# A macaron block with FP4 weights: the decoding of the packed words on 32-bit words instead of 16-bit ones

## The reference, cut to what matters

```python
def dequant_fp4(packed_i32, scales_f16, group_size):   # packed: [out, in/8]
    w = packed_i32.astype(uint32)
    nib = w[:, :, None] >> (arange(8) * 4) & 15        # eight 4-bit codes in a word
    vals = FP4_LUT[nib].reshape(out_f, in_p * 8)       # 0 .5 1 1.5 2 3 4 6, and their negatives
    return vals * repeat(scales_f16.T, group_size, axis=1)

def ffn(x, gate_up_packed, gate_up_scales, down_packed, down_scales):   # inner size 1408
    w_gu, w_down = dequant_fp4(gate_up ...), dequant_fp4(down ...)
    gate, up = split(x @ w_gu.T)
    y = (silu(gate) * up) @ w_down.T
    return y / sqrt(mean(y * y) + 1e-6)

x = X + 0.5 * ffn(layernorm(X), ...)
x = x + attention(layernorm(x), ...)
x = x + 0.5 * ffn(layernorm(x), ...)
```

## Time and profile before

| | |
|---|---|
| median of 3 runs | 2764.01 us (2751.09 to 2766.40) |
| profiled execution | 2762.66 us, its span 2760.8 us |
| mean granted TensorE clock | 0.983 |
| PE busy | 2596.6 us (94%) |
| DVE busy | 1894.5 us (69%) |
| POOL busy | 1574.8 us (57%) |
| ACT busy | 1476.6 us (53%) |

### The profile page before, as it was taken

The page is one execution under the profiler, slowest core; times in us unless marked ns, Lnnn a source line. Parts: engine busy times, 40 slices in busy tenths (PEclk is TensorE's granted clock), DMA queues, the critical chain, the costliest instruction groups (busy, mean ns, idle before and its releaser), DMA issues.

```text
span 2760.8 us, 39357 instructions
## 1 busy us (share of the span) xinstructions
PE 2596.6 (94%) x14559; PEld 1365.0 (49%) x14559; DVE 1894.5 (69%) x3325; ACT 1476.6 (53%) x2823; POOL 1574.8 (57%) x1095
## 2 busy tenths in 40 slices
PE   5799999997998999999999999999999999999997
PEld 3455555554873333333378633333334555555554
DVE  7877777766648777777175487777662777777764
ACT  4366666665222656656622146666665456666664
POOL 4556666665221666666742136666677456666665
PEclk8899999998999999999999999999999999999999
DMA  2002311121122020200050310202003401111101
GB/s 62 1 31 92 126 47 46 46 77 56 36 69 58 4 50 5 63 5 3 15 186 31 79 33 5 48 5 63 5 4 119 175 16 46 47 46 47 46 31 46
DMA packets 75710, 136.32 MB, mean 49 GB/s; under 512 B 18783, under 2 KB 22394, under 8 KB 75390
## 3 DMA queue, kind: packets, MB, share of 16 engines
q1 hardware_dynamic: 75518, 133.81, 15.7%
HBM read 71.12 MB, written 34.34 MB: 38 GB/s over the span
## 4 chain that ended last, share of the span: by engine, by line
PE 69%; DVE 11%; POOL 6%; ACT 4%; issue 4%; SPq 1%; DMA 0%; POOLq 0%; ACTq 0%; DVEq 0%
PE pp L95 54%; PE ps L95 14%; DVE sb L116 6%; POOL sb L104 6%; ACT sb L101 4%; DVE sb L110 3%; SPq L137 1%; DVE sb L104 1%; PE ps L98 1%; DVE sb L107 0%; DMA sb<-sb 0%; PE pp L98 0%; DVE sb L113 0%; DVE sb L122 0%; ACT L101 0%
## 5 line engine op out<-in xcount | busy, mean ns | idle before, releaser
L95 PE MATMUL pp<-sb,sb 128*128 128x512 f32 (+9 forms) x11082 | 2198.1, 440 | 65.7 <-DVE sb L110 17.1
L104 POOL TENSOR_TENSOR sb<-sb,sb 128x512 f32<-128x512 f32 (+6 forms) x1078 | 1567.2, 1475 | 1182.8 <-PE pp L95 442.5
L95 PEld LDWEIGHTS pp<-sb,sb 128*128 128x128 f32 (+4 forms) x11082 | 1075.8, 132 | 931.2 <-issue 383.1
L101 ACT ACTIVATE sb<-pp 128x512 f32<-128x512 f32 (+5 forms) x1382 | 657.6, 550 | 460.1 <-PE pp L95 440.1
L95 PE MATMUL ps<-sb,sb 128*128 128x512 f16 (+7 forms) x2934 | 757.6, 347 | 56.8 <-DVE sb L110 20.2
L101 ACT ACTIVATE sb<-sb 128x512 f32<-128x512 f32 (+4 forms) x500 | 308.1, 620 | 535.2 <-DVE sb L110 362.9
L116 DVE TENSOR_REDUCE sb<-ps 128x1 f32<-128x512 f32 (+3 forms) x754 | 480.2, 668 | 147.9 <-PE ps L95 145.9
L95 PEld LDWEIGHTS ps<-sb,sb 128*128 128x128 f16 (+4 forms) x2934 | 245.8, 101 | 400.3 <-DVE sb L116 108.6
L110 DVE SCALAR_TENSOR_TENSOR sb<-ps,sb,sb 128x512 f32<-128x512 f32 x437 | 320.4, 747 | 135.8 <-PE ps L95 103.6
L110 DVE SCALAR_TENSOR_TENSOR sb<-pp,sb,sb 128x512 f32<-128x512 f32 x443 | 321.5, 745 | 111.7 <-PE pp L95 108.8
L116 DVE TENSOR_REDUCE sb<-pp 128x1 f32<-128x512 f32 (+2 forms) x366 | 242.4, 662 | 88.5 <-PE pp L95 87.1
(11 more groups left out here) (25 smaller groups left out, 379.8 us busy)
## 6 DMA issues: line engine op xcount, KB each, us to landing
sb<-sb SPq DMA_DIRECT2D x192, 128.0 KB, 2.4
sb<-L_attn_X SPq DMA_DIRECT2D x64, 256.0 KB, 3.5
sb<-xa SPq DMA_DIRECT2D x64, 256.0 KB, 4.8
sb<-xc SPq DMA_DIRECT2D x64, 256.0 KB, 3.5
xa<-sb SPq DMA_DIRECT2D x32, 256.0 KB, 2.0
xc<-sb SPq DMA_DIRECT2D x32, 256.0 KB, 5.0
out<-sb SPq DMA_DIRECT2D x32, 256.0 KB, 2.0
dd<-sb SPq DMA_DIRECT2D x11, 512.0 KB, 5.1
```

Source lines behind the costliest of these rows:

```text
L95: return self.e.matmul(*a, **k) if self.e else self
L101: return self.e.activation(*a, **k) if self.e else self
L104: return self.e.tensor_tensor(*a, **k) if self.e else self
```

## The change

The decoding of a chunk stays twelve DVE instructions in the same order. `pk`, `t1` and `vv` are now read and written as 32-bit words, so an instruction has 192 elements in place of 384. The eight tensor_scalar become scalar_tensor_tensor: the shift is still an immediate, while the mask is a second tensor, one 32-bit word (the 16-bit mask twice) read again for every element. The four tensor_tensor become scalar_tensor_tensor too, with a shift by 0 ahead of the OR. POOL fills the masks with two memsets ahead of its other constants, and DVE waits for them once, before the first decoding. `masks` takes 32 bytes of the constants' memory.

```diff
@@ constants
         self.two14 = take([128, 4], F32, 16)
+        self.masks = take([128, 4], U16, 16)
@@ def decode_dve(e, p, f, i):
-    u = p.pk[:, :, :].rearrange("p a b -> p (a b)").bitcast(U16)[:, 384 * i:384 * i + 384]
+    u = p.pk[:, :, :].rearrange("p a b -> p (a b)").bitcast(U32)[:, 192 * i:192 * i + 192]
+    sign, size = (p.masks[:, 2 * j:2 * j + 2].bitcast(U32).broadcast_to([128, 192]) for j in range(2))
+    if i == 0:
+        e.wait_ge(*p.set_signals.at("masks"))
...
             e.wait_ge(*p.V.now())
-            e.tensor_scalar(p.t1[m % 2][:, :], u, 12 - 4 * m, 0x8000, ALU.logical_shift_left,
-                            ALU.bitwise_and).then_inc(*p.V.up())
+            e.scalar_tensor_tensor(p.t1[m % 2][:, :].bitcast(U32), u, 12 - 4 * m, sign, ALU.logical_shift_left,
+                                   ALU.bitwise_and).then_inc(*p.V.up())
             yield
             sh = 9 - 4 * m
-            e.tensor_scalar(p.vv[:, m, half], u, abs(sh), 0x0E00,
-                            ALU.logical_shift_left if sh >= 0 else ALU.logical_shift_right,
-                            ALU.bitwise_and).then_inc(*p.V.up(("bits", i, m)))
+            e.scalar_tensor_tensor(p.vv[:, m, half].bitcast(U32), u, abs(sh), size,
+                                   ALU.logical_shift_left if sh >= 0 else ALU.logical_shift_right,
+                                   ALU.bitwise_and).then_inc(*p.V.up(("bits", i, m)))
             yield
         if m >= 1:
-            v = p.vv[:, m - 1, half]
+            v = p.vv[:, m - 1, half].bitcast(U32)
             e.wait_ge(*p.V.at(("bits", i, m - 1)))
-            e.tensor_tensor(v, v, p.t1[(m - 1) % 2][:, :], ALU.bitwise_or).then_inc(*p.V.up())
+            e.scalar_tensor_tensor(v, v, 0, p.t1[(m - 1) % 2][:, :].bitcast(U32), ALU.logical_shift_left,
+                                   ALU.bitwise_or).then_inc(*p.V.up())
@@ def ffn_pool
+        e.memset(p.masks[:, 0:2], 0x8000).then_inc(*c.up())
+        e.memset(p.masks[:, 2:4], 0x0E00).then_inc(*c.up("masks"))
         e.memset(p.idf[:, :], 0.0).then_inc(*c.up("i0"))
```

More of the change, by code:

```diff
@@ L9 @@
 U16 = mybir.dt.uint16
+U32 = mybir.dt.uint32
 ALU = mybir.AluOpType
```

## The result

The changed kernel takes 2768.32 us (median of 20 runs, 2763.81 to 2770.25), the kernel before 2759.57 (20 runs, 2750.12 to 2766.64). The ratio is 1.0035, interval [1.0024, 1.0046]: slower by some 9.7 us (the two medians are 8.8 apart), inside the 0.5% that the forecast called the same, and inside its range. The forecast was 2770.

The account below looks back on a forecast made before the run. DVE was taken to bound the decoding stretch, PE the kernel from 160 us on. Added path costs of 2.5, 3.3 and 0.4 us made 6.2, taking 2762.66 to 2768.9; 1.35 for the median gave 2770, range 2756 to 2790.

Parts of the forecast that it names:

- The price of one new instruction: DVE's decoding: 156 ns fixed plus 192 x 1.03 gives 354 ns, 0.10 us over an old tensor_scalar.
- Rival B: DVE's new instructions: second operand costs a second cycle, 552 ns each, 24.3 us in sum, time 2788; chance 0.15.
- Rival D: DVE's decoding: half the elements means half the streaming, 4.4 us less, time 2760; chance 0.03.
- The ORs cost nothing: Four ORs per decoding: nothing changes, as the old tensor_tensor took 0.34 us unblocked against 0.354 for the new form.
- The waits for POOL stay: Decoding beside POOL's burst: new instructions still wait for POOL, and the difference is the same 0.10 us as without POOL.
- Rival C: First four of a spread decoding: POOL no longer holds them up, 25 us less on the path, 2739; chance 0.04.
- Decodings 0 and 1: Ahead of DVE's turn of the first tile: all twelve instructions on the path, 0.104 us more per masked one.
- The place: Eight spread decodings: first four masked instructions on the path cost 3.3 us; the other four are mostly covered by DVE's idle time.
- The sum of 6.2 us: Decoding stage: 2.5 us for decodings 0 to 2, 3.3 in eight chunks, 0.4 without cover; afterwards all is a shift.
- The clock: Decoding stage, granted clock 1.2 to 2.4 GHz: two chunks more or fewer at the lower level, 4 us either way.
- Rival E: Spread decodings: one more collision with POOL per chunk, 8 x 1.1 = 9 us on top of 6, 2779; chance 0.06.
- The start point: Whole kernel: profiled execution's 2762.66 us, with the median of the runs shown 1.35 above it, as the time before.

Follow-up runs that it names:

- upper group: No change: of the kernel before's 20 runs, the nine between 2763.4 and 2766.6 us; the trace behind the prediction is one of these.
- the lower: No change: of the kernel before's 20 runs, the nine between 2750.1 and 2754.7 us; one later traced took 2754.74 us.
- zeros: PE makes eight zero products ahead of c = 3 per chunk, first token tile: kernel before 2755.55 us, changed kernel 2768.81, ratio between them 1.0034.

## Why the prediction was right, and what it missed

- The price of one new instruction, 0.354 us from the rows of a small and a large neighbour, came out: of the 132, 101 were not held up by POOL and took 0.35 on average. Rival B is out. Of the two places of the Trainium skill's "Vector Engine (DVE) Microarchitecture Reference" that spoke for it, the first ("Points that are easy to get wrong", two SBUF sources not of bf16 halve the throughput) would have given 0.55 by the forecast's estimate, and the second (5.2, single words at a port) 0.49; neither showed for this form, and the measurement decides.
- Rival D is out by the same number. The copy trick of the Trainium skill's "VectorE: DVE Perf Modes" (its section on the errata) halves the elements, but this form gave up the quicker streaming of the old one with it: the old one took 0.25 us for 384, the new one 0.35 for 192.
- The ORs cost nothing: right, shown by themselves.
- The waits for POOL stay, with 0.10 more each: right, 31 of the new ones waited (32 of the old). Rival C is out.
- Decodings 0 and 1: 16 x 0.104 = 1.7 us forecast; 9.52 us against 7.94 (12.98 to 20.92 before), 1.6 measured.
- The place: right. 32 instructions on the path cost, 32 beside PE do not, 9.6 us apart. But the reason is only in part the 0.10 us each.
- The sum of 6.2 us: the span gave 6.2, in part by luck. Behind the stage the difference was 4.6, and 1.6 came later. Within it the terms stand where they were measured one by one (1.6 for the first two decodings, 0.40 between two evacuations), but the chunks did not grow by 0.4 each: the changed kernel's long ones take 13.6 us, those of before 14.0, as the clock was down for less of them (0.87 against 0.76). Against the upper group the medians give 4.8, in place of 6.2.
- What failed is the step around the sum: that one profiled execution stands for the kernel. Against the upper group, at about 2763.5, the change costs 4.8 us; against the lower, at about 2752, it costs 16; half and half gives about 10, and 9.7 were measured. The clock was taken as 4 us either way, when it makes two courses of 10.5 and 14 us per chunk, and the change closes the shorter one. The trace before had a sign of it, in the chunk that the earlier trace rows are from. By stretch, and the first four instructions of its decoding:

```profile
95.04:105.80 10.76, 8.23 (x43) 5.15 (x42) 10.65 (x22) 4.83 (x10) 7.03 (x6) 1.00 0.01 2
```

```profile
95.80 1.99 DVE L107 TENSOR_SCALAR sb<-sb 128x384 uint16<-128x384 uint16 x4
```

  The four took 1.99 us in place of 5.03, and not because the clock was up, which it also was in the chunk ahead with its 5.03, but because DVE started 0.57 us ahead of the burst (95.80 and 96.37). I had read the short chunks as the work of the clock alone.
- Rival E had the mechanism, one more collision with POOL per chunk at 1.1 us, but put it on the long course, where it did not happen. It happens in the short one: with zeros in both kernels such a chunk grew by 1.36 us, where E's terms come to 1.5 (0.4 and 1.1). As it meets only the chunks of the short course, the whole is 2768 and not E's 2779. Its size per chunk was about right and its chance of 0.06 too low.
- The start point was off as well: the median of three runs, 2764.01, lies 4.4 us above that of twenty. That and the missed cost (3.5 us by the ratio, 2.5 by the medians) go against each other, so that 2770 looks better than it is.

Not shown: what makes the clock fall in one chunk and not in another, and so which course a run of the kernel before takes. PE's longer idle time in the long course is one reading. Against it as the whole cause stands the chunk with 3.81 us idle at a clock of 1.00, and in the last two chunks with a decoding the long course came in spite of the zeros.

## What to carry to other kernels

A wider word halves the elements, but here the form with two tensor inputs took about 1.03 ns for each of its 192, and the one-input form that it replaced some 0.24 ns for each of its 384 (0.09 us above the fixed part); count both before packing. Where two engines take turns at something, ask for the head start as well as for the duration: here 0.57 us let three short instructions start or two longer ones, and 0.1 us more each cost a whole wait of about 1.1. When the few times given already spread over 15 us, look for two courses before trusting the trace of one.

## What the runs showed of the hardware

- scalar_tensor_tensor with both tensors in SBUF, integer and bitwise: 0.35 us for 192 elements of 32 bits, 0.55 for 384 of 16 bits with one mask element read again. About 1.03 ns per element either way, above a fixed 0.156 us.
- tensor_scalar over 192 words of 32 bits, mask as a word per partition: 0.31 us, so at most 0.8 ns per word above the same fixed part.
- Where DVE's and POOL's instructions take turns, POOL is held up too, and more by longer ones: its burst of five took 6.71 us beside four new instructions and 6.41 beside four old; its burst of four took 5.40 beside the new ones and 6.12 beside those over 384 elements (masks as a tensor on 16-bit words).
- The order decides how many waits there are: a decoding that starts 0.57 us ahead of POOL's burst has two waits (old form) or three (new form); one that starts 0.59 us behind it has four, at a granted clock of 1.00.
- The granted clock stayed at 1.00 over four chunks in which PE idled some 1.9 us each for the evacuation of c = 2, and over one in which it idled 3.81; it fell in the changed kernel's chunk with 3.42. So this idle time alone does not tell when it falls.
